# A four-layer graph network on one core: blocks that end without GpSimd's drain, semaphores cleared in three scopes, and a third row buffer in layer 0

## What is computed

```python
# layer 0: transformer attention, 4 heads of 16
scores = einsum('ehd,ehd->eh', q[src], k[dst]) / sqrt(16)
agg    = segment_sum(softmax_by_segment(scores, dst)[:, :, None] * v[src], dst)
gate   = sigmoid(concat([skip, agg, skip - agg]) @ Wg + bg)
out    = prelu(layernorm(gate * skip + (1 - gate) * agg))
# layer 1: 2 heads over x[src] + bond, a softmax, then batch norm and relu
# layer 2: 1 head, q from two edge arrays, k and message from x[src] and a third
# layer 3: a message network without attention, a mean over the edges, an update network
```

## Time and profile before

| | us |
|---|---|
| median of 3 runs | 9189.79 (9188.56 to 9192.16) |
| the profiled execution's own time | 9190.77 |
| its span, first to last instruction | 9188.4 |
| POOL busy | 6641.2 (72%) |
| DVE busy | 4742.3 (52%) |
| ACT busy | 3299.8 (36%) |
| PE busy | 2848.2 (31%) |

### The profile page before, as it was taken

How to read it: one execution, slowest core, us unless ns; L and a number is a source line. 1 busy time by engine, 2 the same in 40 slices (tenths; PEclk the granted TensorE clock), 3 DMA queues, 4 the chain that set the end, 5 groups by cost and what they waited for, 6 DMA issues and landing times. The chain is left out here.

```text
span 9188.4 us, 65012 instructions
## 1 busy us (share of the span) xinstructions
PE 2848.2 (31%) x15711; PEld 2538.8 (28%) x15711; DVE 4742.3 (52%) x6653; ACT 3299.8 (36%) x4404; POOL 6641.2 (72%) x6982
## 2 busy tenths in 40 slices
PE   2000000000110000000035666666654555555555
PEld 1000000000110000000025666666644555555554
DVE  5365656565757777777735444454545222222224
ACT  0132323232212232323224555555545444444442
POOL 6677777777677777777747777777765777777775
PEclk6555555555555555555558888888875555555555
DMA  8233333333123333333313434344421333333322
GB/s 352 72 106 109 106 109 105 110 105 101 29 66 112 100 112 100 112 100 112 96 54 131 139 124 139 127 135 131 132 83 50 87 97 88 96 94 89 97 87 71
DMA packets 365617, 979.47 MB, mean 107 GB/s; under 512 B 163732, under 2 KB 173102, under 8 KB 350916
## 3 DMA queue, kind: packets, MB, share of 16 engines
q1 hardware_dynamic: 134852, 667.04, 19.5%
q0 software_dynamic: 224608, 290.88, 13.8%
q10 hardware_dynamic: 6048, 20.52, 0.6%
HBM read 579.27 MB, written 398.69 MB: 106 GB/s over the span
## 5 line engine op out<-in xcount | busy, mean ns | idle before, releaser
L739 POOL DMA_INDIRECT qv<-qv_table,edge_ix x1512 | 1427.1, 944 | 492.7 <-issue 481.8
L739 POOL DMA_INDIRECT g<-x_table,edge_ix x1512 | 1427.1, 944 | 483.3 <-issue 480.2
L739 POOL DMA_INDIRECT se<-x_table,edge_ix x1512 | 1427.3, 944 | 460.7 <-issue 460.7
L739 POOL DMA_INDIRECT comb<-x_table,edge_ix x1512 | 1427.2, 944 | 460.6 <-issue 460.6
L810 DVE TENSOR_TENSOR_SCAN edge_val<-edge_bank,edge_val 128x464 f32<-128x464 f32 (+1 forms) x728 | 699.9, 1031 | 1440.5 <-ACT edge_val L1438 1434.0
L820 ACT ACTIVATE edge_sums<-edge_val 128x1904 f32<-128x1904 f32 (+3 forms) x220 | 1114.9, 5068 | 0.0
L1406 PE MATMUL h_ps<-w_hidden,edge_comb_t 97*128 97x128 f32 x3136 | 759.6, 422 | 202.2 <-ACT edge_comb_t L1433 202.2
L795 ACT ACTIVATE edge_bank<-edge_weight_arg 128x112 f32<-128x112 f32 (+2 forms) x168 | 38.4, 229 | 2170.9 <-DVE edge_decay_arg L789 2170.9
L1406 PEld LDWEIGHTS h_ps<-w_hidden,edge_comb_t 97*128 97x128 f32 x3136 | 701.6, 328 | 237.9 <-ACT edge_comb_t L1433 237.7
L810 DVE TENSOR_TENSOR_SCAN edge_val<-edge_decay,edge_val 128x493 f32<-128x493 f32 (+1 forms) x672 | 714.0, 1131 | 13.4
L930 PE MATMUL edge_k_ps<-ident,edge_fix_wide 128*128 128x128 f32 x8 | 2.1, 441 | 2134.3 <-DVEq L890 2134.3
(11 more groups left out here) (394 smaller groups left out, 8667.2 us busy)
## 6 DMA issues: line engine op xcount, KB each, us to landing
sums<-edge_sums SPq DMA_DIRECT2D x56, 1848.0 KB
sums<-edge_sums SPq DMA_DIRECT2D x56, 1792.0 KB, 7.1
sums<-edge_sums SPq DMA_DIRECT2D x56, 1008.0 KB, 4.3
sums<-edge_sums SPq DMA_DIRECT2D x56, 924.0 KB, 3.7
edge_k<-k_edges SPq DMA_DIRECT2D x56, 896.0 KB, 4.6
edge_bond<-in_edge_attr SPq DMA_DIRECT2D x56, 896.0 KB
edge_eh<-in_edge_attr SPq DMA_DIRECT2D x56, 896.0 KB
edge_qr<-in_edge_attr_n SPq DMA_DIRECT2D x56, 896.0 KB
```

The costliest lines, as they stand in the source:

```text
L739: e.indirect_dma_start(self.gather_into(b, j), None, self.gather_from, bass.IndirectOffsetOnAxis(ap=now[:, j:j + 1], axis=0))\
```

## The change

Six edits.

```diff
-        self.first_src = keep("first_src", [P, 2 * J], U32)
+        self.first_src = keep("first_src", [P, 3 * J], U32)
...
-        block = ctx.enter_context(nc.Block())
+        block = ctx.enter_context(nc.Block(no_gpsimd_drain=True))
...
-            load(e, p.first_src[:, :], ins["src"][:, 0:2 * J])
+            load(e, p.first_src[:, :], ins["src"][:, 0:3 * J])
...
-        self.gathered = [[gathered[b]] if self.begun else [self.sem(f"gathered{b}_{c}") for c in range(parts)]
-                         for b in (0, 1)]
+        self.gathered = [[sem] for sem in gathered] if self.begun else \
+            [[self.sem(f"gathered{b}_{c}") for c in range(parts)] for b in (0, 1)]
+        self.alone = 2 if self.begun else 0
...
-        with e.Fori(0, self.rounds - 1) as i:
+
+        def turn(i):
...
+        for i in range(self.alone):
+            turn(i)
+        with e.Fori(self.alone, self.rounds - 1) as i:
+            turn(i)
...
-                now = self.index[b][:, :] if i else self.p.first_src[:, b * J:(b + 1) * J]
-                if i:
+                n = 2 * i + b
+                u = self.buffer(i, b)[0]
+                now = self.index[b][:, :] if n >= len(self.gathered) else self.p.first_src[:, n * J:(n + 1) * J]
+                if n >= len(self.gathered):
                     e.wait_ge(self.index_in[b], 16 * i)
-                    e.wait_ge(self.rows_free[b], i + 1)
+                    if self.begun and n in (3, 4):
+                        e.wait_ge(self.rows_free[1 - b], 2)
+                    else:
+                        e.wait_ge(self.rows_free[b], i + 1)
...
+    def buffer(self, i, b):
+
+        if not self.begun:
+            return b, (i, 1, 1)
+        if isinstance(i, int) and i < 2:
+            return ((0, (0, 0, 1)), (1, (0, 0, 1)), (2, (0, 0, 1)), (0, (0, 0, 2)))[2 * i + b]
+        return 1 - b, (i, 1, b)
...
-    def gpsimd(self, e):
+    def gpsimd(self, e, drained=False):
         ph = self.ph
+        if drained:
+            e.drain()
...
-            with e.Fori(0, ph.rounds) as i:
+
+            def chunks(i):
...
+            for i in range(ph.alone):
+                chunks(i)
+            with e.Fori(ph.alone, ph.rounds) as i:
+                chunks(i)
...
+            e.dma_start(p.x[:, :, :], p.ins["x"].rearrange("(p t) f -> p t f", p=P)).then_inc(x_again, 16)
             i = ph.rounds - 1
...
             chained.scalar(e)
+            e.wait_ge(x_again, 16)
...
-    with nc.reset_on_exit(), ExitStack() as ctx:
+    with ExitStack() as ctx:
...
             ph.gpsimd(e)
-            chained.gpsimd(e)
+            chained.gpsimd(e, drained=True)
...
             ph.gather(e)
+            e.drain()
...
-        with nc.reset_on_exit(), ExitStack() as sems:
-            p.qv_tiles = [sems.enter_context(nc.sbuf_tensor(f"qv{b}", [P, J, 2 * FD], F32)) for b in (0, 1)]
-            p.qv_gathered = [sems.enter_context(nc.semaphore(f"qv_gathered{b}")) for b in (0, 1)]
-            p.k_all = sems.enter_context(nc.sbuf_tensor("k_all", [P, p.nodes_pp, FD], F32))
-            p.firsts = sems.enter_context(nc.sbuf_tensor("k_firsts", [P, FD], F32))
+        with nc.reset_on_exit(), ExitStack() as sems, ExitStack() as rows:
+            p.qv_tiles = [rows.enter_context(nc.sbuf_tensor(f"qv{b}", [P, J, 2 * FD], F32)) for b in range(3)]
+            p.qv_gathered = [sems.enter_context(nc.semaphore(f"qv_gathered{b}")) for b in range(3)]
+            p.k_all = p.x
+            p.firsts = rows.enter_context(nc.sbuf_tensor("k_firsts", [P, FD], F32))
...
             edge_phase_0(p)
-        node_phase_0(p)
-        edge_phase_1(p)
-        node_phase_1(p)
-        edge_phase_2(p)
-        node_phase_2(p)
-        edge_phase_3(p)
-        node_phase_3(p)
+            rows.close()
+            node_phase_0(p)
+            edge_phase_1(p)
+        with nc.reset_on_exit():
+            node_phase_1(p)
+            edge_phase_2(p)
+            node_phase_2(p)
+        with nc.reset_on_exit():
+            edge_phase_3(p)
+            node_phase_3(p)
```

More of the change, by code:

```diff
@@ L731, in gpsimd @@
             for b in (0, 1):
-                now = self.index[b][:, :] if i else self.p.first_src[:, b * J:(b + 1) * J]
-                if i:
+                n = 2 * i + b
+                u = self.buffer(i, b)[0]
+                now = self.index[b][:, :] if n >= len(self.gathered) else self.p.first_src[:, n * J:(n + 1) * J]
+                if n >= len(self.gathered):
                     e.wait_ge(self.index_in[b], 16 * i)
-                    e.wait_ge(self.rows_free[b], i + 1)
+                    if self.begun and n in (3, 4):
+                        e.wait_ge(self.rows_free[1 - b], 2)
+                    else:
+                        e.wait_ge(self.rows_free[b], i + 1)
                 for j in range(J):
-                    if 2 * J * i + J * b + j < done:
+                    if J * n + j < done:
                         continue
-                    e.indirect_dma_start(self.gather_into(b, j), None, self.gather_from,
+                    e.indirect_dma_start(self.gather_into(u, j), None, self.gather_from,
                                          bass.IndirectOffsetOnAxis(ap=now[:, j:j + 1], axis=0))\
-                        .then_inc(self.gathered[b][j * self.parts // J], 16)
+                        .then_inc(self.gathered[u][j * self.parts // J], 16)
+    def buffer(self, i, b):
[4 more added lines that the diff above has]
+        return 1 - b, (i, 1, b)
     def wait_part(self, e, i, b, c):
-        columns = J // self.parts
-        e.wait_ge(self.gathered[b][c], at(i, 16 * columns, 16 * columns))
+        u, (times, per, more) = self.buffer(i, b)
+        columns = 16 * J // self.parts
+        e.wait_ge(self.gathered[u][c], at(times, per * columns, more * columns))
     def wait_gathered(self, e, i, b):
@@ L984, in _ @@
             ph.clear_carries(e)
-            with e.Fori(0, ph.rounds) as i:
+            def chunks(i):
                 for b in (0, 1):
-                    q = tiles[b][:, :, 0:FD].rearrange("p j f -> p f j")
+                    rows_now = tiles[ph.buffer(i, b)[0]]
+                    q = rows_now[:, :, 0:FD].rearrange("p j f -> p f j")
                     e.wait_ge(k_turned, at(i, 2, 1 + b))
@@ L1011, in _ @@
                     ph.wait_weights(e, i, b)
-                    v = tiles[b][:, :, FD:].rearrange("p j (h d) -> p h d j", h=4)
+                    v = rows_now[:, :, FD:].rearrange("p j (h d) -> p h d j", h=4)
                     for n in range(4):
```

4 lines of the change are left out of this document (2 added, 2 removed).

## The result

The changed kernel takes **9127.63 us** (median of 4 runs, 9125.01 to 9131.42), beside 9189.17 for the kernel before (4 runs, 9186.70 to 9192.16): a ratio of 0.9933, 95% interval 0.9916 to 0.9950. That is 61.5 us less, where 55.2 were forecast; the interval leaves 1 out, so the kernel is faster, by 0.7%. The profiled execution has a span of 9129.7 us and took 9131.42.

A forecast was written before the change was run, and what follows sets the result against it. POOL's indirect transfers were taken to set the time in edge phases, so gains lay in its breaks. Terms summed to 59.7 us, less 4.5 for x, 55.2: forecast 9134.6 us, range 9126 to 9149.

The forecast's parts named there:

- A: End of search: POOL's DRAIN gone, only the barrier and the way to the first gather left; 8.2 us won.
- B: Third row buffer: POOL's 10.67 us wait for chunk 0's buffer becomes 0.30; 10.4 us won.
- C: End of edges 0: DRAIN and clearing gone, one barrier stays; 8.9 us won.
- D: End of nodes 0: DRAIN and clearing gone, one barrier stays; 10.6 us won.
- G and I: Ends of edges 2 and edges 3: DRAIN and clearing gone, one barrier stays; 9.9 us won each.
- Term E: End of edges 1: clearing stays, its DRAIN taken as 2.50 us; gain 0, between +2.5 and -6.3.
- Term F: End of nodes 1: only the clearing goes, the DRAIN being hidden under node arithmetic; 1.8 us won.
- Term X: Second load of x, late in edges 0: contention holds up a POOL gather; 4.5 us lost, bounds 0 and 6.4.
- Rival 1: Gathers behind five block ends take over a 5.8 us stall each, 29 us of gain lost; 9163 us, chance 9%.
- Rival 2: A DRAIN's work must be done, or the DRAIN stays; 9174 us, chance 6%.
- Rival 3: Third buffer gains nothing: DVE or SP is late next, or unrolled rounds stall; 9145 us, chance 8%.
- Rival 4: Without DRAINs each indirect transfer gets dearer, 61 ns more in edges 1 and edges 2; 9325 us, chance 4%.

The follow-up runs named there:

- buffer alone: The kernel before with only the third row buffer, two rounds written out and x loaded twice; all DRAINs and clearings kept: 9180.23 us beside 9190.32.
- split DRAINs: The changed kernel with two more DRAINs in nodes 3, behind 14 and 42 of its 98 gathers: 12315.51 us beside 12370.21, on a slower chip.
- late drains: The changed kernel without its three written-out DRAINs in edges 1, nodes 2 and nodes 3; the clearings' own DRAINs remain: 9151.67 us.
- no drain alone: The kernel before with `no_gpsimd_drain=True` in all ten blocks, all eight clearings kept: 9206.87 us, ratio 1.0018.
- DRAINs back: The changed kernel with POOL's DRAIN back in all ten blocks, all else kept: 9165.78 us, ratio 0.9974.

## Why the prediction was right, and where its steps were not

The forecast of 9134.6 us stands 7.0 above the 9127.6 measured, in its range of 9126 to 9149, with its main sum right: the DRAINs and clearings went at the places and at the prices that it named. What it had wrong partly cancelled, and that is luck: 5.9 and 1.9 us more gained at the ends of edges 1 and edges 2, 1.1 and 4.8 us more lost by x and in nodes 3. By its own steps:

**Terms A, B, C, D, G and I** held. A came to 9.0 for 8.2: the step took the 1.1 us from the DRAIN's end to the first gather as a remainder, but without the DRAIN POOL's sequencer does the barrier at 326.2, 15 us before the last scatter ends, and only 0.30 stays. B 10.4 for 10.4, C 9.0 for 8.9, D 10.5 for 10.6, G 9.9 and I 9.6 for 9.9 each. Chunks 3 and 4 have no wait, as reckoned, though the margin of chunk 3's index is 404 - 387.8 = 16 us and not "24 us or more". On the slower chips chunk 5 does wait, 14.6 to 15.4 us with x loaded late, where the kernel before with seven semaphores waits 10.6 and 10.8 at chunk 2; there the third buffer moves the wait. And B and C overlap: of C's 9.0 the buffer alone had brought 4.6, since it left a DRAIN of 2.51 in that place.

**Term E** was mis-sized: 2.75 for 0. The step took "the 2.50 of the same place" for the clearing's DRAIN, between 0.03 and 8.80. What decides is how many transfers were made since the DRAIN before, and here they were two, the fix row's gather and scatter: 0.22. The runs with late and split DRAINs show this. The 1.9 us ahead of the fix row's scatter were in no term: the early DRAIN took away a break that the prediction hadn't seen, so it is worth some 4.7 us in all, counting the 2.75. The waits for the last sums, 1.2 us shorter in edges 1 and 1.9 in edges 2, aren't the change's: the one in edges 2 is 27.2 to 27.3 us in some runs (before, buffer alone, late drains) and 25.4 in others (after, no drain alone, DRAINs back), and the one in edges 1 is 37.5 to 37.6 in all of these but before, where it is 38.68.

**Term F**, the end of nodes 1, was 0.6 for 1.8, and the end of nodes 2, which the prediction put at 0, was 1.3. Both ends hang on the node arithmetic: in the kernel before, POOL's DRAIN behind nodes 1 ends at 4789.6 and SP's, the last, starts at 4836.3. The second moved by as much though its clearing stayed, and a microsecond of one profile can't be told apart from that.

**Term X** had the size, 5.6 for 4.5, and the wrong mechanism. The step said "a gather of POOL can be held up" and took the earlier trace rows as its price. No gather got longer: the 3.88 and 3.01 at the head of edges 1 and the 7.34 at the head of edges 2 are those of before. What x met was one of POOL's regular breaks. Of the 5.6 us, 1.8 are such a break more (13 for 12 in edges 0) and 3.8 are this one's length. That it was x which stretched it has three supports. The times: x lands at 2237.4 and POOL resumes 2.8 us later, and in the three other runs with the stop it is 2.7 to 2.8. The slower chips: the same break, with the buffer and without x under way, is 2.23 us in six runs. And edges 1 there: these breaks are 4.1 to 5.9 us where a store of 1848 KB was issued 1.0 to 3.5 us ahead. On a chip where the stop exists x wasn't moved alone. That the size came out at all is luck, for the 4.5 was scaled from long gathers of another kind. The prediction's "in the steady state ... there is nothing of this: mean 944 ns" looked at the duration of a gather, and the breaks are idle time: the page has 481.8 and 480.2 us of idle time ended by "issue" for edges 0 and edges 1, beside the 460.7 of edges 2 in the earlier trace rows:

```profile
L739 POOL DMA_INDIRECT qv<-qv_table,edge_ix x1512 | 1427.1, 944 | 492.7 <-issue 481.8
```

**Rival 1**, the stall moving into the gathers, is out: behind A, C, D, G and I the first transfers take 0.96 to 0.99 us, and the mean stays at 944 ns. What the single long transfers come from isn't shown: those of 7.34 and 6.94 us stand where they stood, and no run moved the first of them. **Rival 2**, that the work of a DRAIN must be done, was put at 6%, and its core is true: no run without DRAINs in the blocks got rid of the work, and the run with the flag alone was 16.5 us slower. The changed kernel escapes since it merges scopes, so that the DRAINs of ten blocks become three of 9.2 us, and puts these under waits that exist anyway. Without those two parts the flag loses. The time was right because the prediction counted the clearings' places one by one, not because it knew why the DRAIN is long. **Rival 3** is out by the 0.30 at chunk 2. **Rival 4** is out: the gathers still take 944 ns, though no DRAIN stands between the first 3533 transfers.

The last 4.8 us, in nodes 3 and behind, were in no term: two gathers of 1.86 us, each with one of 1.15 behind it, and 2.4 us more between the last gather and the end. The second half isn't the change's: that stretch is 24.7 us in the run with the buffer alone and 22.3 with the DRAINs back, beside 22.3 before and 24.8 after.

## What to carry to other kernels

GpSimd's DRAIN behind indirect transfers was mostly a debt here, not a wait (8.05 us, more than 50 us after the last of them): dropping it from the blocks' ends gained only where no other DRAIN, such as a semaphore clearing's, followed in the open, and alone it cost 16.5 us. Put one DRAIN under a long wait that exists anyway, as the 9.2 us were put under 37.52 here, and leave as few transfers as possible between it and the clearing (two here, and 0.22 us). Before adding a load to a tuned phase, look for the regular short stops of the engine that sets the time: here the gathers beside 3136 KB of x kept their 0.94 us, and the stop of 2.1 us that x met was 5.93.

## What the hardware showed that was not expected

A DRAIN of POOL took 0.22 us after 2 indirect transfers, 2.75 after 28, 4.6 after 56, 8.06 after 98, and 9.2 after 1584 and more, even where the last of them had ended 50 us earlier. In edges 0 a regular break starts this count anew (7.08 us for 85 transfers behind it, 2.51 for 29). No run here shows what the DRAIN does with the transfers that it counts.

In edge phases POOL stops for 2.0 us every 112 gathers where all gathers of a buffer count on one semaphore, and has no such stop where they count on two or seven. With a store of 1848 KB issued 1 to 3.5 us ahead the stop was 4.1 to 5.9 us. And three chips took 12335 to 12370 us for a kernel that another runs in 9190. In edges 2 a gather cost the same there, 943 ns, but in edges 1 1027 to 944. SP's issue of a store in edges 1 took 1.40 us (median of 54) where the other chip has 0.36; in edges 2 and edges 3 it was 0.36 there too. And the idle time ended by "issue" was longer: 1429.1 us before one group of PE's where it was 19.1.
